# Shared tiles' gates ahead of the last routing, low halves of the weights split between two engines' spare stretches, six shared results kept

## What is computed

```python
h = layernorm(x) * (1 + ca) + sa
x = x + ga * attention(h, w_qkv, w_out)      # 16 heads of 16, window 64
h = layernorm(x) * (1 + cb) + sb
scores = abs((h @ ru_w.T) * silu(h @ rg_w.T))
probs = softmax(scores)                       # 16 experts
idx = top_k(probs + extra_bias, 4)
for e in range(16):                           # only tokens that chose e count
    y += silu(h @ Wg[e].T) * (h @ Wu[e].T) @ Wd[e].T * coeff[:, e]
z = silu(h @ Sg.T) * (h @ Su.T) @ Sd.T        # shared expert, all tokens
x = x + gb * (y + z)
```

## Time and profile before

| | us |
|---|---|
| median of 3 runs | 564.14 (559.98 to 564.74) |
| the profiled execution, its own time | 557.91 |
| its span in the profile | 556.1 |
| PE busy | 503.4 (91%) |
| DVE busy | 380.4 (68%) |
| POOL busy | 301.1 (54%) |
| ACT busy | 281.0 (51%) |

### The profile page before, as it was taken

The page is one execution under the profiler, slowest core; times in us unless marked ns, Lnnn a source line. Parts: engine busy times, 40 slices in busy tenths (PEclk is TensorE's granted clock), DMA queues, the critical chain, the costliest instruction groups (busy, mean ns, idle before and its releaser), DMA issues.

```text
span 556.1 us, 11906 instructions
## 1 busy us (share of the span) xinstructions
PE 503.4 (91%) x3457; PEld 462.8 (83%) x3457; DVE 380.4 (68%) x1051; ACT 281.0 (51%) x735; POOL 301.1 (54%) x261
## 2 busy tenths in 40 slices
PE   2699999999999998999878787899999999999966
PEld 0589998999898898989655576789999999999956
DVE  6769952545768678686777668977677677777443
ACT  2358764464445545444463446455556555564311
POOL 6546611010225464354657539987766676677671
PEclk9999999999899999999777899999999999999979
DMA  7556996689678485642367447557777886776586
GB/s 195 150 164 215 259 304 193 176 216 221 179 235 252 145 242 162 195 126 75 123 231 237 149 126 163 88 104 133 130 122 129 198 129 128 129 130 111 103 260 151
DMA packets 72499, 94.23 MB, mean 169 GB/s; under 512 B 9339, under 2 KB 61882, under 8 KB 72118
## 3 DMA queue, kind: packets, MB, share of 16 engines
q1 hardware_dynamic: 53368, 60.35, 40.2%
q0 software_dynamic: 16384, 27.32, 23.9%
q10 hardware_dynamic: 2686, 5.81, 3.5%
HBM read 57.27 MB, written 41.88 MB: 178 GB/s over the span
## 4 chain that ended last, share of the span: by engine, by line
PE 65%; DVE 15%; issue 7%; DMA 6%; POOL 4%; ACT 2%; SPq 0%; DVEq 0%; POOLq 0%; ACTq 0%
PE GU_e L108 12%; PE YP_e L108 11%; PE O L1402 8%; PE QB L108 5%; PE VB L108 4%; PE TB L1392 3%; PE SB L1380 3%; PE HT_e L1982 3%; PE XT_e L1972 3%; POOL acc L1846 2%; PE TB L1390 2%; DMA acc<-h,ids_st 2%; PE SB L1377 2%; DVE lo L194 2%; PE Y L1419 2%
## 5 line engine op out<-in xcount | busy, mean ns | idle before, releaser
L1846 POOL DMA_INDIRECT acc<-h,ids_st x59 | 93.4, 1583 | 38.4 <-DMA acc<-h,ids_st 15.0
L143 POOL DMA_INDIRECT xs_scr<-h,slot_u x64 | 63.0, 984 | 62.0 <-PE TB L1392 25.3
L108 PE MATMUL GU_e<-gu_hi,xT 128*128 x316 | 82.6, 343 | 1.5 <-DVE xT L1873 0.8
L108 PE MATMUL YP_e<-dn_hi,aT 88*128 x316 | 67.6, 306 | 6.0 <-DVE aT L1878 6.0
L1772 ACT ACTIVATE aT<-HT_e 88x256 fp32r<-88x256 f32 (+1 forms) x89 | 34.9, 394 | 69.1 <-PE HT_e L1982 69.1
L949 ACT ACTIVATE prob<-TB 128x512 f32<-128x512 f32 x64 | 38.2, 597 | 58.2 <-PE TB L1392 57.4
L1402 PE MATMUL O<-raw,prob 128*128 128x99 f32 x512 | 67.1, 278 | 0.0
L1402 PEld LDWEIGHTS O<-raw,prob 128*128 128x128 f32 x512 | 62.4, 194 | 0.1
L1885 DVE TENSOR_TENSOR h_act<-GU_e,g_act 128x176 f32<-128x176 f32 (+1 forms) x89 | 32.0, 360 | 43.5 <-ACT g_act L1765 42.5
L108 PEld LDWEIGHTS YP_e<-dn_hi,aT 88*128 88x128 f32 x316 | 47.8, 188 | 13.0 <-issue 9.3
L108 PEld LDWEIGHTS GU_e<-gu_hi,xT 128*128 128x128 f32 x316 | 51.1, 189 | 2.1 <-issue 2.0
(11 more groups left out here) (245 smaller groups left out, 1221.9 us busy)
## 6 DMA issues: line engine op xcount, KB each, us to landing
x_st<-xs_scr SPq DMA_DIRECT2D x79, 144.0 KB
dn_hi<-k_scr SPq DMA_DIRECT2D x48, 192.0 KB, 3.9
k_scr<-raw SPq DMA_DIRECT2D x8, 768.0 KB, 6.1
dn_hi<-q_scr SPq DMA_DIRECT2D x24, 256.0 KB, 4.4
q_scr<-raw SPq DMA_DIRECT2D x8, 512.0 KB, 3.6
raw<-in_egu SPq DMA_DIRECT2D x8, 352.0 KB
raw<-in_x SPq DMA_DIRECT2D x16, 128.0 KB, 3.9
x_res<-in_x SPq DMA_DIRECT2D x32, 64.0 KB, 3.3
```

Of the source, the lines that this page charges most:

```text
L108: mm = eng.matmul(out, a, b, start=(i + j == 0), stop=(i == len(pairs) - 1 and j == 2))
L143: eng.indirect_dma_start(T["xs_scr"], bass.IndirectOffsetOnAxis(ap=T["slot_u"][:, par, t % 2, k:k + 1], axis=0), T["h2"][:, row, :], None) ...
L1846: eng.indirect_dma_start(acc, bass.IndirectOffsetOnAxis(ap=ids_st[:, r:r + 1].bitcast(U32), axis=0), results(r % 8), None, compute_op=ALU. ...
```

## The change

- ACT: the first two shared tiles' SILUs come before the split of expert 3 and the last pair's routing; the exponential's table is then loaded by a dummy activation (`exp_first`); the third SILU and first `tail_aT` follow the routing's exponentials, ahead of the splits of experts 6 to 8 and of the padding.
- DVE: the first two gates come ahead of the last pair's `route_scores`; low halves 0 and 1 ahead of the residual of the last tile; low halves 2 to 5 within the table work, all before the second `tail_out`; the others from step 3 on.
- TensorE: the fourth gate-and-up and the first transpose come ahead of the last pair's ranks, with a wait for DVE's reading of the router's bank.
- POOL: 13 low halves in one run ahead of the scatters instead of 5, the other three after scatters 8, 10 and 12; it issues no plain loads between scatters any more.
- SP: issues those loads instead (raw weights of experts 13 to 15, and later the shared expert's weights), after a wait for the tail's stored sums.
- The end: six results are kept instead of three, added in two parts (tiles 0 to 3, then 4 and 5), and the stores have another order.

The core of the diff:

```diff
-HI_AHEAD, LO_AHEAD, DN_AHEAD = 13, 5, 5
+HI_AHEAD, LO_AHEAD, DN_AHEAD = 13, 6, 13
-LOW_STEPS = (0, 1, 3, 4, 5, 7, 8, 9, 11, 12, 13)
+LOW_STEPS = (3, 4, 5, 7, 8, 9, 11, 12, 13, 14)
...
         normalise_x1(PAIRS - 1, 1)
+        tail_silu(0)
+        tail_silu(1)
         split_hi(eng, T, 3)
+        h2_out(PAIRS - 1)
+        eng.wait_ge(first, 2)
+        eng.activation(exp_first[:, 1:2], exp_first[:, 0:1], ACT.Exp)
         split_hi(eng, T, 4)
-        h2_out(PAIRS - 1)
         split_hi(eng, T, 5)
-        split_hi(eng, T, 6)
         router_exp(PAIRS - 1, 0)
         router_exp(PAIRS - 1, 1)
-
-        tail_silu(0)
-        tail_silu(1)
+        tail_silu(2)
+        tail_aT(0)
+        split_hi(eng, T, 6)
         split_hi(eng, T, 7)
...
         route_scores(PAIRS - 2)
+        gu_low(eng, T, 0)
+        gu_low(eng, T, 1)
         residual(LAST, 3, im, PAIRS - 1)
...
         place(PAIRS - 2)
+        tail_gate(0)
+        tail_gate(1)
         route_scores(PAIRS - 1)
...
         place(PAIRS - 1)
-        tail_gate(0)
-        tail_gate(1)
         steps_of_experts()
-        gu_low(eng, T, 0)
+        gu_low(eng, T, 2)
         tail_gate(2)
         steps_table()
+        gu_low(eng, T, 3)
         tail_out(0)
-        gu_low(eng, T, 1)
         tail_gate(3)
+        gu_low(eng, T, 4)
         table_out()
-        gu_low(eng, T, 2)
+        gu_low(eng, T, 5)
         tail_out(1)
         tail_gate(4)
-        gu_low(eng, T, 3)
...
         tail_gate_up(2)
+        tail_gate_up(3)
+        eng.wait_ge(r_dve, R_OPS * (PAIRS - 1) + 7)
+        tail_transpose(0)
         ranks(PAIRS - 1, 1, SB[1][:, 2 * NE:4 * NE])
...
-        tail_transpose(0)
-        tail_gate_up(3)
...
-    KEPT = 3
+    KEPT = 6
...
+        eng.wait_ge(ty_mm, NB)
+        eng.wait_ge(z_keep, 8 * NB)
+
         def step(s, r, i, first, last):
+            if s < NE - HI_AHEAD:
+                load_raw(eng, A, T, HI_AHEAD + s, HI_AHEAD + s + 1, w_last[s])
+            if s == NS - 40:
+                eng.dma_start(sgu_raw[:, :, :, :], A["sgu"]).then_inc(sgu_ld, 16)
+                eng.dma_start(sdn_raw[:, :, :], A["sd"]).then_inc(sdn_ld, 16)
...
-        eng.wait_ge(final, 2)
+        eng.wait_ge(final, 1)
+        store_out(0)
         store_out(1)
-        store_out(0)
-        eng.wait_ge(final, 3)
-        store_out(2)
         eng.wait_ge(fold, 3)
         store_out(5)
+        for k, g in enumerate((3, 2)):
+            eng.wait_ge(final, k + 2)
+            store_out(g)
...
         for e in range(DN_AHEAD):
             dn_low(e)
-        eng.wait_ge(ty_mm, NB)
-        eng.wait_ge(z_keep, 8 * NB)
-        load_raw(eng, A, T, HI_AHEAD, HI_AHEAD + 1, w_last[0])
-        eng.wait_ge(step_tab, 1)
...
-            if s < NE - DN_AHEAD:
-                dn_low(DN_AHEAD + s)
-            if s in (1, 2):
-                load_raw(eng, A, T, HI_AHEAD + s, HI_AHEAD + s + 1, w_last[s])
...
+            if s in (8, 10, 12):
+                dn_low(HI_AHEAD + s // 2 - 4)
...
-            if n == 6:
-                add_kept()
+            if n == 8:
+                add_kept(0, 4)
+            if n == 9:
+                add_kept(4, 6)
```

More of the change, by code:

```diff
@@ L708, in attention_and_routing @@
     mT = sb("mT", [HEADS, 2, P], F32R)
+    exp_first = sb("exp_first", [P, 2])
     rden = sb("rden", [P, 2, 8])
@@ L1031, in _ @@
         fill_up(nc, eng, A, T, 11, 13)
-        tail_aT(0)
-        tail_silu(2)
         fill_up(nc, eng, A, T, 13, 14)
@@ L1287, in table_out @@
             eng.tensor_copy(step_i[:, :, :], SB[1][0:1, 0:2 * P].rearrange("p (a x) -> p a x", a=2)).then_inc(step_tab, 1)
+        eng.memset(exp_first[:, :], 0.0).then_inc(first, 1)
         eng.memset(msum[:, 0, 0, :].bitcast(F32), 0.0).then_inc(first, 1)
@@ L1358, in _ @@
         tail_out(3)
-        gu_low(eng, T, 4)
         tail_out(4)
@@ L1747, in _ @@
         store_out(7)
-        for g in (3, 4):
-            eng.wait_ge(final, g + 1)
-            store_out(g)
+        eng.wait_ge(final, 4)
+        store_out(4)
         eng.wait_ge(o_out, 16 * TILES)
@@ L1847, in step @@
                                    None, compute_op=ALU.add).then_inc(sent[s % 2], 16)
-            if s < NE - DN_AHEAD:
-                dn_low(DN_AHEAD + s)
-            if s in (1, 2):
-                load_raw(eng, A, T, HI_AHEAD + s, HI_AHEAD + s + 1, w_last[s])
-            if s == NS - 40:
-                eng.dma_start(sgu_raw[:, :, :, :], A["sgu"]).then_inc(sgu_ld, 16)
-                eng.dma_start(sdn_raw[:, :, :], A["sd"]).then_inc(sdn_ld, 16)
+            if s in (8, 10, 12):
+                dn_low(HI_AHEAD + s // 2 - 4)
         for_steps(eng, step, NS)
@@ L1906, in add_late, with add_kept @@
             done.then_inc(final if n % 2 else z_late, 1)
-        def add_kept():
+        def add_kept(low, high):
             eng.wait_ge(z_late, KEPT)
-            eng.wait_ge(fold, 1)
-            eng.tensor_tensor(to_add[:, 0:KEPT, :], to_add[:, 0:KEPT, :], z_kept[:, 0:KEPT, :], ALU.add).then_inc(final, 1)
+            eng.wait_ge(fold, (high - 1) // 4 + 1)
+            eng.tensor_tensor(to_add[:, low:high, :], to_add[:, low:high, :], z_kept[:, low:high, :], ALU.add).then_inc(final, 1)
         x_lo(0, 0)
@@ L2109, in program @@
             T["odd_sums"] = last_use.enter_context(nc.sbuf_tensor("odd_sums", [P, TILES, D], F32))
-            T["z_kept"] = last_use.enter_context(nc.sbuf_tensor("z_kept", [P, 4, D], F32))
+            T["z_kept"] = last_use.enter_context(nc.sbuf_tensor("z_kept", [P, 6, D], F32))
         with ExitStack() as early:
```

## The result

| | before | after |
|---|---|---|
| median, us (12 runs each, measured together) | 561.97 | 569.83 |
| ratio to before, 95% interval | | 1.0256 [1.0194, 1.0318] |
| profiled execution, own time, us | 557.91 | 564.4 |
| its span, us | 556.1 | 562.4 |

The changed kernel is slower. The forecast was 552.5 us, faster, with a range that ended at 562. (The ratios go by the shorter executions of each kernel, of which the kernel before has one of 547.59 us here, so that this one says more than the 1.4% between the medians; of the kernels marked * in the last table, the trace is of a longer execution.) The two traces differ by 6.3 us of span.

What follows compares the result with a forecast made beforehand. It saw DVE low halves held by POOL's in tail and early steps, and a fold wait at the end. Span 548.0 against 556.1 gave 549.8, then 552.5 us with half the gap to the median; range 543 to 562.

Steps and rivals of the forecast that it cites:

- tail: End of attention, 262 to 322 us: ends at 320.2, a gain of 2.3 us, bounds 4.1 and -0.7.
- steps up to 18: Early expert steps: 7.4 us won less 0.7, 3.1 and 0.7, a gain of 2.9, bounds 7.4 and -6.
- 18 to first shared tile: Expert steps from 18 on: no gain of their own; first shared tile moves from 505.44 to 500.2 by earlier gains.
- end: Shared tiles and stores: 8.3 us of waiting go if folds are in time, but stores wait for an addition; span 548.0.
- The steps: Sixteen early expert steps at 2.21 us plus 0.11 for a DVE low half: 37.1 us instead of 44.6.
- three other waits: Signs of a wrong forecast: a many-us low half, transposes waiting over 5 us at steps 2 to 4, folds releasing DVE.
- the collisions: Early steps: POOL's low halves of experts 13 to 15 meet DVE's, three at 1.4 us, half hidden, counted as -0.7.
- half of 6.2 on 549.8: Final sum: profiled execution lay 6.2 us under the median; half carried over onto 549.8, giving 552.5.
- The stall at x tile 4: Early steps: tile 4 issued behind SP's raw loads stalls up to 2.5 us; 3.1 in all, 0.7 for the clock.
- Rival 3: Raw loads before x tiles 4 to 6 hold SP's queue for their whole landing: time 561 us; chance 0.20.
- ring order: Early steps: descriptors consumed in ring order put tile 4 behind 528 KB of raw bytes: stall 4.6, forecast 1.5 us higher.
- margin against POOL's run: Tail: DVE's low half 5 starts 2 us before POOL's thirteen; rival 4, missing it, costs 16 us, chance 0.08.

Runs made afterwards that it cites:

- low halves two ahead: Changed kernel with DVE's low halves of experts 12 to 15 made one step earlier each (steps 10 to 13): 553.1 us beside 563.6, ratio 0.992.
- both edits: Changed kernel with low halves of experts 12 to 15 one step earlier and x tiles ahead of raw loads: 550.08 us beside 563.6, ratio 0.9863.
- old end with both edits: Changed kernel with earlier low halves and x tiles first, but the end of the kernel before (three results kept): 551.5 us beside 564.45, ratio 0.983.

## Why the prediction was wrong

The forecast's terms beside the two traces, in us gained:

| term | forecast | measured | low halves two ahead | both edits |
|---|---|---|---|---|
| tail | 2.3 | 1.4 | 2.4 | 3.2 |
| steps up to 18 | 2.9 | -11.3 | -0.9 | 3.2 |
| 18 to first shared tile | 0 | -0.4 | -0.2 | -0.3 |
| end | 2.9 | 3.0 | 2.5 | 2.1 |
| sum | 8.1 | -7.4 | 3.8 | 8.3 |

**The step that failed** is "The steps", where sixteen steps were put at 37.1 us: a step's length on TensorE plus 0.11 for a low half on DVE. That prices a low half by DVE's time for it and never asks when it is due. The old and the new `LOW_STEPS` stood side by side in the text, and from `LO_AHEAD` plus the position in the list one reads that expert 12 loses two steps of lead and experts 13 to 15 one. That put a wait of 1.8 to 2.5 us and a lower clock into four steps in a row: 12.3 us, from 30.2 to 17.9 when they were made one step earlier. None of the rivals held it either, and the list of what would show the forecast wrong named three other waits. The trace of the kernel before had a sign of it, in step 15 with a low half two steps ahead:

```profile
363.46 0.58 PE L108 MATMUL GU_e<-gu_hi,xT 128*128 x2 [0.68 <-DVE lo L194]
```

**In the same step the gain was sized too high.** With low halves two steps ahead, and the x tiles as forecast, the stretch up to step 18 is 0.9 us longer than before. The stall there is 4.1 us, so 3.3 were won, where 6.7 were counted (7.4 less the collisions). By the starts of DVE's gating, steps 5 to 10, with low halves in most of them and none of POOL's, take 2.1 to 2.9 us, 2.5 in the mean, and not 2.3. And the kernel before lost less by collisions than it seemed: of its steps 2 to 15 eight take 3.0 to 3.7 us, but the other six, in which it catches up, 1.3 to 2.4. Two sums in that step are also wrong as written: 0.11 belongs to the ten steps with a low half and not to sixteen (36.5 us, not 37.1), and three collisions at 1.4, half hidden, are 2.1 and not 0.7. With both edits steps 11 to 14, with two collisions, take 11.0 us where four steps of 2.3 are 9.2, so 0.9 for each. In the sum, half of 6.2 on 549.8 gives 552.9, not 552.5.

**The stall at x tile 4** was right in its sum: 3.1 and 0.7 for the clock forecast, 3.48 + 0.24 + 0.19 = 3.9 measured at tiles 4 to 6, and 2.7 to 4.1 us come back in the stretch up to step 11 when the tiles go first. Nearly all of it is tile 4, which had up to 2.5 in the forecast. Rival 3 (a whole landing for each of three tiles) is refuted. By the ring order of the Trainium skill (DMA: Bandwidth & Descriptors, Queues, rings and completion order) I had put the stall at 4.6; the measurement lies between that and the sum's 3.1, and no run here separates order from shared bandwidth.

**The tail** was about right in its sum and its parts: no gain before the table, 2.1 us of margin against POOL's run, and a price of 14 us in the tail when that margin is given away. The gates' own move brings nothing that shows.

**The end** was right in its sum (2.9 and 3.0) and in its chain (the addition, then sixteen stores, 12.8 us), but not in its cause. Given POOL's scatters earlier, the old end ends as early or earlier. What decides is the lag of the last scatter, 7.6 us behind the first shared tile in the changed kernel instead of 12.2. The forecast had the scatter come earlier too, but never asked what the old end would do then; that six kept results were needed was argued from the old lag.

## What to carry to other kernels

When work that feeds a loop is moved, list for each piece the step in which it is made and the step that waits for it, before and after; a piece that stands behind waits for the same step's matmuls needs a lead of two or more here, because with one the loop goes round in series (with two, waits of 0.7 us stayed, with three none). Where a wait is set for the worst case of the data, the step that counts is the one in the wait. And a term that fits can hide a wrong cause, as the end's did: undo each part by itself before crediting it.

## What was not expected of the hardware

DVE's subtraction was held through twelve consecutive subtractions of POOL (15.39 us against 0.88), and got through only when POOL paused; in two traces it was held through five though it had started 0.50 us ahead of the first; the five of the kernel before were no accident. The granted clock fell to 0.72 in a stretch in which TensorE waited about 2 us in every 5 to 6, so that 6.5 us more of waits cost 12.3. And the start of the tail lies at 272.9 us in the changed kernel's trace and at 280.4 in that of the old end with both edits, whose code up to there is the same.
